# Layer-norm coefficients of the first layer over two turns instead of four, and the first softmax chunk one score iteration sooner

## The reference

```python
h = jnp.maximum(_layernorm(x, axis=-1), 0.0)
x = x + _L0_gnn_ref(h, L0_gnn_W, adj, L0_gnn_bias)    # diagonal, upper and lower part of adj, three weights
h = jnp.maximum(_layernorm(x, axis=-1), 0.0)
x = x + _L1_gnn_ref(h, adj, ...)                      # normalised adj, 128->256->128, two batch norms
h = jnp.maximum(_layernorm(x, axis=-1), 0.0)
x = x + _L2_gnn_ref(h, adj, ...)                      # two graph convolutions, then LSTMs over windows of 1 to 4
h = jnp.maximum(_layernorm(x, axis=-1), 0.0)
x = x + _L3_gnn_ref(h, ..., adj, src, dst)            # attention over 256 edges, 4 heads
```

## Time and profile before

| what | value |
| --- | --- |
| median of 3 runs | 1243.06 us (1242.41 to 1245.5) |
| the profiled execution's own time | 1244.22 us |
| its span, first to last instruction | 1242.4 us |
| mean granted TensorE clock | 0.993 of full |
| busy: PE, DVE, ACT, POOL | 1200.0, 995.2, 899.0, 365.2 us |

### The profile page before, as it was taken

One profiled execution on the slowest core, in us unless ns is written; L12 is line 12 of the kernel. 1 busy time (PEld: TensorE's weight loads), 2 busy tenths in 40 slices (PEclk: granted clock), 3 DMA queues, 4 the chain that ended last, 5 costly groups with the idle time before them and its releaser, 6 DMA issues.

```text
span 1242.4 us, 22221 instructions
## 1 busy us (share of the span) xinstructions
PE 1200.0 (97%) x7198; PEld 1014.5 (82%) x7198; DVE 995.2 (80%) x2019; ACT 899.0 (72%) x1737; POOL 365.2 (29%) x676
## 2 busy tenths in 40 slices
PE   8988999999999998899999999999999999989998
PEld 8988895663398887679887987898889899977997
DVE  5877768997768885898879887988777799987774
ACT  5756658868658885887788777877777588874554
POOL 5657631000067440000000000000000277757774
PEclk9989999999999999999999999999999999999999
DMA  8000000000031110000000000000300030001212
GB/s 317 1 1 1 2 1 0 0 1 0 0 136 68 68 68 1 1 1 1 1 1 1 1 1 1 1 1 1 136 1 2 1 137 1 2 2 43 77 69 85
DMA packets 14921, 38.20 MB, mean 31 GB/s; under 512 B 1904, under 2 KB 3952, under 8 KB 13808
## 3 DMA queue, kind: packets, MB, share of 16 engines
q1 hardware_dynamic: 14000, 36.60, 7.7%
q10 hardware_dynamic: 832, 0.46, 0.2%
HBM read 20.27 MB, written 16.78 MB: 30 GB/s over the span
## 4 chain that ended last, share of the span: by engine, by line
PE 42%; DVE 12%; ACT 3%; issue 2%; POOL 1%; POOLq 0%; DVEq 0%; ACTq 0%
PE psum L1151 7%; PE psum L1150 7%; PE psum L1152 7%; PE psum L1169 5%; PE psum L1165 4%; PE psum L1166 4%; DVE l_M L1486 3%; PE psum L1686 2%; PE psum L1651 2%; PE psum L1661 2%; ACT gates L1188 2%; DVE l2r_st L116 2%; DVE X L1333 1%; PE psum L1672 1%; DVE scores L1355 1%
## 5 line engine op out<-in xcount | busy, mean ns | idle before, releaser
L1188 ACT ACTIVATE gates<-psum,lstm_bias 128x512 f32<-128x512 f32 (+1 forms) x504 | 302.3, 637 | 100.9 <-PE psum L1169 88.5
L175 ACT ACTIVATE l_h<-X,nmr,rstd 128x128 f32<-128x128 f32 (+1 forms) x512 | 209.9, 484 | 39.0 <-POOLq L169 26.8
L143 POOL TENSOR_TENSOR l2r_sum<-l2r_st 128x8 f32<-128x8 f32 x16 | 5.2, 322 | 517.3 <-DVE l2r_st L116 517.0
L1151 PE MATMUL psum<-lstm_node_hi,Wih_lo 128*128 128x512 f32 (+1 forms) x408 | 148.3, 364 | 0.0
L1150 PE MATMUL psum<-lstm_node_hi,Wih_hi 128*128 128x512 f32 (+1 forms) x408 | 148.0, 363 | 0.0
L1152 PE MATMUL psum<-lstm_node_lo,Wih_hi 128*128 128x512 f32 (+1 forms) x408 | 147.9, 363 | 0.0
L1165 PE MATMUL psum<-lstm_hid_hi,Whh_hi 128*128 128x512 f32 (+1 forms) x288 | 104.6, 363 | 3.9 <-DVE lstm_hid_hi L1248 3.7
L1169 PE MATMUL psum<-lstm_hid_lo,Whh_hi 128*128 128x512 f32 (+1 forms) x288 | 108.0, 375 | 0.0
L1166 PE MATMUL psum<-lstm_hid_hi,Whh_lo 128*128 128x512 f32 (+1 forms) x288 | 103.7, 360 | 0.0
L1193 ACT ACTIVATE gates<-lstm_cell 128x512 f32<-128x512 f32 (+1 forms) x144 | 83.7, 581 | 21.0 <-DVE lstm_cell L1235 20.6
L1150 PEld LDWEIGHTS psum<-lstm_node_hi,Wih_hi 128*128 128x128 f32 x408 | 77.2, 189 | 10.8 <-ACT gates L1188 0.3
(11 more groups left out here) (266 smaller groups left out, 3279.1 us busy)
## 6 DMA issues: line engine op xcount, KB each, us to landing
x_spill<-X SPq DMA_DIRECT2D x32, 256.0 KB, 2.0
X<-x_spill SPq DMA_DIRECT2D x2, 4096.0 KB, 13.8
out<-X SPq DMA_DIRECT2D x32, 256.0 KB, 2.0
X<-in_x SPq DMA_DIRECT2D x6, 1024.0 KB, 15.9
X<-in_x SPq DMA_DIRECT2D x3, 512.0 KB, 8.0
w_raw<-in_WihT SPq DMA_DIRECT2D x1, 1024.0 KB, 5.3
w_raw<-in_WhhT SPq DMA_DIRECT2D x1, 1024.0 KB, 8.1
X<-in_x SPq DMA_DIRECT2D x2, 256.0 KB, 3.4
```

What stands on the lines that cost most here:

```text
L175: last = act.activation(h[:, j, :], k.X[:, bass.ds(b0, TB), :][:, j, :], ACT.Relu, bias=k.nmr[:, bass.ds(b0, TB)][:, j:j + 1], scale=k.rst ...
L1151: pe.matmul(out, lo, x_high, start=False, stop=False)
L1188: act.activation(gate_of(it, g), k.bank[4 * s + g][:, 0:it.N], ACT.Tanh if g == GATE_G else ACT.Sigmoid, bias=k.lstm_bias[:, it.p - 1, g:g ...
```

## The change

Three edits. (1) `L0_TURNS` goes from 4 to 2: the next layer's chain is 16 columns wide and runs in turns 2, 4, ..., 14, right behind turn i's bias and ahead of `x_ln.coefficients(i + AHEAD)`; the eighth chain runs in the hidden stage. (2) The hardware loop of the hidden stage is cut in two halves, and ACT waits for that last chain between them, at tile 16, instead of ahead of tile 4. (3) In the scores all steps of chunk 0's softmax move one iteration ahead (13 and 14 instead of 14 and 15); the head sum of iteration 13 goes behind `keep_exponential`; `high` of tiles 0 and 1 moves from the end of iteration 13 to the end of 14, `load_exponential` the other way; POOL's `low` of tiles 0 and 1 moves from before iteration 14's halvings to before 15's; and `low` of tile 2 moves from behind the last halving to between the last two.

```diff
-L0_TURNS = 4
+L0_TURNS = 2
@@ stage_first, POOL
                 pool.tensor_tensor(out=tile(i, 1), ...).then_inc(biased[1], 1)
+                if i and i % L0_TURNS == 0:
+                    ln.coefficients(pool, i // L0_TURNS - 1)
                 if i + AHEAD < n_it:
                     x_ln.coefficients(pool, i + AHEAD)
-                if i % L0_TURNS == L0_TURNS - 1 and i < n_it - 1:
-                    ln.coefficients(pool, i // L0_TURNS)
@@ stage_gcn_hidden
-    def steps(eng, step):
+    def steps(eng, step, between=None):
         for t in range(-S, 2 * S):
             step(t, t % S)
-        with eng.Fori(2, n_it - 1) as i:
-            for s in range(S):
-                step(i * S + s, s)
+        for first, end in ((2, n_it // 2), (n_it // 2, n_it - 1)):
+            with eng.Fori(first, end) as i:
+                for s in range(S):
+                    step(i * S + s, s)
+            if between:
+                between()
+                between = None
@@ its ACT
-                if isinstance(t, int) and t == 2 * S - 1:
-                    k.l0_ln.wait(act, 0, n_it // L0_TURNS - 1)
...
-            steps(act, step)
+            steps(act, step, lambda: k.l0_ln.wait(act, 0, n_it // L0_TURNS - 1))
@@ Scores.on_pool
-            if i == n_it - 2:
+            if i == n_it - 1:
                 for t in range(2):
                     at.low(pool, t)
             for s in range(S):
                 self.halve(pool, i, s)
+                if i == n_it - 1 and s == 0:
+                    at.low(pool, 2)
@@ Scores.on_scalar
-            if i == n_it - 1:
+            if i == n_it - 2:
                 at.sm.exponential(act, 0)
...
             if i == n_it - 3:
+                at.sm.load_exponential(act)
+            if i == n_it - 2:
                 for t in range(2):
                     at.high(act, t)
-            if i == n_it - 2:
-                at.sm.load_exponential(act)
@@ Scores.on_tensor: linear_term and turn_in at n_it - 3, turn_back and sum_up at n_it - 2
@@ Scores.on_vector
+            if i == n_it - 3:
+                at.sm.add_linear(dve, 0)
-            if i:
+            if i and i != n_it - 2:
                 self.sum_heads(dve, i - 1)
...
             if i == n_it - 2:
-                at.sm.add_linear(dve, 0)
-            if i == n_it - 1:
                 at.sm.keep_exponential(dve, 0)
+                self.sum_heads(dve, i - 1)
                 at.sm.invert(dve, 0)
...
-                if i == n_it - 1 and s == 0:
-                    at.sm.weigh(dve, 0)
...
-            if i == n_it - 2:
+            if i == n_it - 3:
                 at.sm.score_in(dve, 0)
                 at.sm.max_forward(dve, 0)
                 at.sm.max_backward(dve, 0)
                 at.sm.subtract_max(dve, 0)
+            if i == n_it - 2:
+                at.sm.weigh(dve, 0)
@@ Attend.on_pool
-                if self.there(ahead):
+                if self.there(ahead) and ahead > 2:
```

More of the change, by code:

```diff
@@ L1437, in on_tensor @@
             for s in range(S):
-                if i == n_it - 1 and s == S - 1:
+                if i == n_it - 2 and s == S - 1:
                     at.sm.turn_back(pe, 0)
@@ L1442, in on_tensor @@
                 last.then_inc(R["V"][s], 1)
+            if i == n_it - 3:
+                at.sm.turn_in(pe, 0)
             if i == n_it - 2:
-                at.sm.turn_in(pe, 0)
-            if i == n_it - 1:
                 at.sm.sum_up(pe, 0)
```

## The result

The changed kernel takes 1228.22 us (median of 4 runs, 1227.96 to 1228.64) against 1242.87 (4 runs, 1242.41 to 1245.5): 14.65 us less, ratio 0.9882, 95% interval 0.9866 to 0.9899. The prediction was 1226.7 in a range of 1223 to 1232. The profiled execution took 1227.96 us with a span of 1226.0, which is 16.4 less than before's span.

The account below looks back on a forecast made before the run. TensorE, busy 1200.0 of 1242.4 us, was taken to bound the kernel, so time could come only from its waits and slow-clock stretches. Savings 13.1 + 1.6 + 1.7 = 16.4 us; 1243.06 - 16.4 = 1226.7 us, range 1223 to 1232.

Parts of the forecast that it names:

- Part 1: First layer: 16-column chains behind the bias remove DVE's waits and the three long turns' stalls; 13.1 us saved.
- allowance of 0.5 for lateness: First layer: 0.5 us in sum taken off the saving for chains late by a few tenths.
- Rival C: First layer: clock or short lateness eats half of its second share, leaving 8.7 us saved; 1231 us, chance 0.12.
- straight line for 16 columns: First layer: chain cost interpolated between 8 columns (4.37 us) and 32 (8.87 us), giving 5.87 us.
- Part 2: Hidden stage: ACT's wait for the last chain goes, TensorE's product for tile 4 comes 1.6 us sooner.
- Part 3: Scores: chunk 0's softmax one iteration sooner and low of tile 2 in POOL's hole; 1.7 us saved.
- first link: Scores, iteration 14: normalisation behind the exponential delays q_hi, so l_M comes 4.6 us late.
- 0.5 us for the softmax's place: Scores, iteration 15: l_M 0.6 us sooner, but the gather in TensorE's order holds weighted, so 0.5 us counted.
- rival B: Scores: TensorE's gap of about 2.4 us before sum_up drops the clock in iteration 14; price 1.6 to 3.0, chance 0.1.
- Rival A: Scores: serial ring exponential, norm, q_hi, sum, reciprocal lengthens iteration 14, nothing given back; 1231.8 us, chance 0.16.
- Rival D: Hidden stage: cutting the loop stalls TensorE once or twice, 1.5 to 3 us; 1229 us, chance 0.05.
- The table: Scores, ACT: relu behind the exponential needs no reload; otherwise two more 1.28 us loads, softmax gain about -0.9.

Follow-up runs that it names:

- e4: Changed kernel with the first layer's chain over four turns (32 columns) again, still behind the next turn's bias; 1236.34 us.
- e7: Changed kernel with the hidden stage as before: one uncut loop, ACT's wait ahead of its fourth tile, chain still 16 columns; 1227.99 us.
- part 3 alone: Kernel before with only the scores and the softmax's first chunk changed; 1243.14 us, ratio 0.9994, before in the same session 1243.47.
- e3: Changed kernel with POOL's low(2) back in its old place, behind the weighted_low of the first odd tile; one run, 1229.51 us.
- e9: Changed kernel with ACT's normalisation of iteration 15 ahead of the exponential instead of behind it; 1225.03 us, ratio 0.9854.
- e10: Changed kernel with sum_up behind the edge products of iteration 14 and the reciprocal behind its weighting; 1228.0 us.
- e12: Changed kernel with 9 small unused matmuls on TensorE ahead of sum_up in iteration 14, filling its gap; 1228.68 us.
- e11: Changed kernel with iteration 15's normalisation ahead of the exponential, and sum_up and reciprocal moved behind iteration 14's edge products and weighting; 1225.25 us.

## Why the prediction was right, and where not

- **Part 1, 13.1 us.** Right in mechanism and, for this pair of executions, in size: 12.8 and 0.7 from turn 15. The turns that it rests on came out one by one: 6.26 (said 6.2), 2.68 (2.7) and 4.77 (4.7). The allowance of 0.5 for lateness was 0.9 net: turns 4 and 6 (10.43 and 10.41 us, before 9.63 and 9.67) grew by 1.5, turn 7 shrank by 1.15, turns 10 and 14 grew by 0.3 and 0.2. But the sum took the clock losses of one execution as fixed. Another of the same code has 1.9 us less of them, which leaves 11.5. Rival C named both halves of this, the clock and chains late by some tenths. The lateness is real, but small: it is about the 0.8 us of turn 4, not half of part 1.
- **The straight line for 16 columns.** The power took 2.91 us, near the 2.9 that was said. The chain took 5.6 us in the hidden stage (estimate 5.87), but 5.8 to 6.6 in the first layer: in turn 4 it took 6.3, and two of its small instructions ran 0.61 and 0.52 us instead of 0.21 while DVE worked. ACT's waits for POOL were 0.68 and 0.25 us; both were to be under 0.5.
- **Part 2, 1.6 us.** The number is right (1.63), and moving the wait does earn it where the chain is wide (`e4`). But the prediction did not see that edit (1) already takes the stall away: `e7` keeps the wait and loses nothing. The rows allowed that to be seen: a chain 3.0 us shorter leaves 3.95 - 3.0 = 0.95 us of ACT's wait, measured 0.94, and TensorE had felt only the last 1.46 us of those 3.95.
- **Part 3, 1.7 us, is the step that failed.** Its value was 0.2 us in the profiled pair, 1.2 with the clock up. Its first link held: M(14) late by 4.6 to 5.0, said 4.6; and with the clock up M(15) was 0.3 to 0.4 us sooner, said 0.6. `low` in the hole gave 1.16, said 1.2. The 0.5 us for the softmax's place came out as about 0.1; and rival B happened, at 1.0 us rather than 1.6 to 3.0, in five of the seven profiled executions with this gap (not in part 3 alone and `e3`). Giving it 0.10 was too little: the gap it named (2.4 us, measured 2.33) was in the forecast's own timeline.
- **Rival A** did not win, but its ring was the thing to act on: the prediction counted the normalisation behind the exponential as "new on the path" and did not ask whether it could stand before it.
- **Rival D** and the Trainium skill's "Runtime: NRT & Kernel Launch", section Instruction fetch mechanics, by which a taken branch out of the prefetched window makes the engine wait for a fetch: no stall at either loop shows, 2.61 us a tile across the cut, and cut and uncut loop take 1228.2 and 1228.0 us. Whether these branches leave that window no run shows. **The table**: a relu follows the exponential with no table load between (1088.57 and 1088.89 above), which agrees with the Trainium skill's "ScalarE: Activation LUTs", section Table sets: the hidden batching unit, by which relu is in every set.
- **The total.** By the medians the forecast is 1.5 us low: part 3's missing 1.5. The spans agreed to 0.1 us only because the profiled execution of before lost another 1 us of clock near 520, which nothing in the change touches: of the 16.4 us, 15.1 come up to the end of the hidden stage, about 1.0 between there and M(12), and 0.2 behind it.

## What to carry to other kernels

Try width and place of a helper chain apart: here half the width and the earlier place together removed the long turns of the first layer, each alone only in part (8.1 and 5.6 us short of the two together). At the last wait either the narrow chain or the moved wait was enough, and the second edit was worth nothing; so before restructuring a wait, subtract what the other edit already takes off it. When an in-order engine gets a new blocking step, look at what is ready behind it and fits into the idle time ahead of it. When two executions of one kernel differ in where TensorE's clock fell, sum a saving in waits and in clock separately, and give the clock share a range.

## What the runs showed of the hardware beyond what was expected

- The gap of 2.33 us ahead of `sum_up` was followed by half clock in five of seven profiled executions with the same TensorE program there, the ones of 0.80 (`e9`) and, ahead of the edge products, 1.41 us (`e10`) were not, in one execution each. The price was 1.0 to 1.1 us.
- At the start of the LSTM (495 to 525 us) the granted clock of some 10 us window is below 1.00 in nine of the fourteen profiled executions and in none of the other five: before 0.83 at 515 to 525, after 1.00. It differs even where the code up to there is the same: `e9` 1.00 throughout, `e12` 0.83 at 505 to 515. A difference of 1 us between two traces is therefore to be read stage by stage.
- The same DVE multiplication (`weigh`) took 0.54 us in the changed kernel, beside a halving on POOL (1097.28 to 1099.99), but 1.21 in `e11` and 1.22 in `e10`, beside a `low` on POOL (in `e11` 1097.24 to 1099.92). That POOL caused it was not tested.
